# Where the two masked key tiles stand in a flash-attention strip, and how the evacuation of four accumulators is cut in two

## The reference

```
h = layernorm(x)
q, k, v = h @ Wq.T + bq, h @ Wk.T + bk, h @ Wv.T + bv
s = q @ k.T / 32
w = softmax(where(causal, |s|, -inf))          # score * sign(score) = |score|
x = x + layernorm((w @ v) @ Wo.T + bo)
x = x + layernorm(layernorm(x) @ Wfq + fbias + (layernorm(x) @ a) @ b)
```

## The kernel before, in words

| strip | nt | last pieces, by position |
|---|---|---|
| 1 | 4 | 1: lnattn_a(0), lnattn_b(0); 2: outproj(1), lnattn_a(1), ln2t(0), xa(0); 3: ffn(0), lnattn_b(1), lnffn(0) |
| 2 | 6 | 3: outproj(1), lnattn_a(1); 4: ln2t(0), xa(0), ffn(0), lnattn_b(1); 5: lnffn(0) |
| 3 | 8 | 5: ln2t(0), xa(0); 6: ffn(0), lnattn_b(1), lnffn(0) |
| 4 | 10 | 7: xa(0), ffn(0); 8: lnattn_b(1), lnffn(0) |
| 5 | 12 | 9: ffn(0), lnattn_b(1); 10: lnffn(0) |
| 6, 7, 8 | 14, 16, 18 | lnffn(0) at 11, 13, 15 |
| 9 to 15 | 20 to 32 | lnffn(0) at 16, 18, 20, 21, 23, 25, 26 |

## Time and profile before

### The profile page before, as it was taken

One profiled execution on the slowest core, in us unless ns is written; L12 is line 12 of the kernel. 1 busy time (PEld: TensorE's weight loads), 2 busy tenths in 40 slices (PEclk: granted clock), 3 DMA queues, 4 the chain that ended last, 5 costly groups with the idle time before them and its releaser, 6 DMA issues.

```text
span 3685.8 us, 57317 instructions; the slowest of 8 cores (3636.0 to 3685.8 us)
## 1 busy us (share of the span) xinstructions
PE 2705.2 (73%) x17129; PEld 1633.3 (44%) x17129; DVE 1365.5 (37%) x2102; ACT 1406.2 (38%) x3137; POOL 407.2 (11%) x728
## 2 busy tenths in 40 slices
PE   2279888566777778888837988856677777878884
PEld 1234333233445555566513433323344555556661
DVE  3335555344444333333342112034444433333333
ACT  0055453233333344444414545323333344444441
POOL 0000001000111111111100000000011111111110
PEclk9999999778898999999958999967878999999996
DMA  5622222321322323333313222232132232333330
GB/s 148 200 92 92 88 87 84 108 66 58 100 84 89 106 91 111 111 114 109 95 63 126 81 69 69 77 107 66 51 102 83 87 95 95 118 97 122 107 112 18
DMA packets 96560, 348.18 MB, mean 94 GB/s; under 512 B 16245, under 2 KB 16373, under 8 KB 94858
## 3 DMA queue, kind: packets, MB, share of 16 engines
q0 software_dynamic: 64112, 226.54, 20.0%
q1 hardware_dynamic: 32154, 117.97, 9.7%
HBM read 266.85 MB, written 77.59 MB: 93 GB/s over the span
## 4 chain that ended last, share of the span: by engine, by line
PE 50%; DVE 18%; ACT 17%; issue 8%; DMA 4%; ACTq 1%; DVEq 1%; POOLq 0%; SPq 0%; POOL 0%
PE SBp L491 11%; PE OTp L911 8%; PE OTp L532 6%; PE SBp L870 6%; DVE sqb L195 6%; DVE stats L192 5%; PE LBp L751 4%; PE EB L751 4%; PE EB L639 3%; PE LBp L639 2%; DVE t L661 2%; ACT PT L891 2%; ACT Sa L878 2%; ACT stats L203 2%; ACT stats L201 2%
## 5 line engine op out<-in xcount | busy, mean ns | idle before, releaser
L911 PE MATMUL OTp<-PT,V_buf 128*128 128x256 bf16 x4352 | 627.9, 293 | 369.3 <-ACT PT L891 369.0
L870 PE MATMUL SBp<-Qs,Ktr 128*128 128x256 bf16 x4352 | 611.4, 288 | 114.2 <-DVE rl L609 62.9
L911 PEld LDWEIGHTS OTp<-PT,V_buf 128*128 128x128 bf16 x4352 | 439.7, 104 | 485.6 <-issue 411.7
L491 PE MATMUL SBp<-lnT,wsl 128*128 128x512 bf16 x2048 | 485.6, 402 | 76.9 <-ACT Qs L498 44.0
L870 PEld LDWEIGHTS SBp<-Qs,Ktr 128*128 128x128 bf16 x4352 | 410.6, 102 | 235.9 <-issue 159.6
L932 POOL DMA_DIRECT2D Ktr<-k_scr x544 | 299.5, 551 | 1896.8 <-PE SBp L870 1746.2
L208 DVE TENSOR_TENSOR stats<-stats 128x1 f32<-128x1 f32 x256 | 40.8, 159 | 936.5 <-ACT stats L206 928.3
L491 PEld LDWEIGHTS SBp<-lnT,wsl 128*128 128x128 bf16 x2048 | 207.8, 102 | 349.4 <-issue 137.4
L878 ACT ACTIVATE Sa<-SBp 128x256 f32<-128x256 f32 x544 | 209.1, 384 | 295.2 <-PE SBp L870 261.8
L192 DVE TENSOR_REDUCE stats<-t 128x1 f32<-128x1024 f32 x160 | 195.2, 1220 | 260.5 <-ACT t L766 239.4
L891 ACT ACTIVATE PT<-Sa 128x256 bf16<-128x256 f32 x544 | 226.6, 417 | 155.2 <-ACT Sa L878 91.4
(11 more groups left out here) (110 smaller groups left out, 2752.8 us busy)
## 6 DMA issues: line engine op xcount, KB each, us to landing
Ktr<-k_scr POOLq DMA_DIRECT2D x544, 256.0 KB, 3.0
xb<-x SPq DMA_DIRECT2D x128, 512.0 KB, 3.6
y<-xb POOLq DMA_DIRECT2D x64, 512.0 KB, 3.9
q_scr<-Qs POOLq DMA_DIRECT2D x32, 512.0 KB, 4.7
k_scr<-Ktr POOLq DMA_DIRECT2D x64, 256.0 KB, 2.8
Qs<-q_scr SPq DMA_DIRECT2D x32, 512.0 KB, 5.4
xb<-fk SPq DMA_DIRECT2D x8, 512.0 KB, 5.5
xb<-wo SPq DMA_DIRECT2D x8, 512.0 KB, 6.3
```

Source lines behind the costliest of these rows:

```text
L491: E("tensor", lambda e, wreg=wreg, kc=kc, dc=dc, bk_=bk_: e.matmul(out=SBp[:, bk_ * 512:bk_ * 512 + 512], lhsT=wsl[:, wreg * 8192 + dc * 1 ...
L870: E("tensor", lambda e, pos=pos, dc=dc, sp=sp, qof=qof: e.matmul(out=SBp[:, sp * 512:sp * 512 + 256], lhsT=Ktr[:, (pos % 4) * 1024 + dc * ...
L911: lst=(last and vc % 2 == 1): e.matmul(out=OTp[b_][:, col:col + 256], lhsT=V_buf[:, tile * 1024 + vc * 128:tile * 1024 + (vc + 1) * 128], ...
```

## The change

The reordering of tiles is dropped: position j now holds tile j, so the two diagonal tiles stand at the last two positions of the strip instead of the first two. And `pre` is cut: `t_rl` and the evacuations of accumulators 0 and 1 stay at the strip's start, those of accumulators 2 and 3 (`pre2`) are issued behind `emit_S(0)`. The core of the diff; `pos` is renamed `j` throughout.

```
-                for b_ in range(4):
+                for b_ in range(2):
                     pre.append(t_otevac(b_))
+                pre2 = [t_otevac(2), t_otevac(3)]
...
-                    if tile >= 2 * s:
-                        r = E("vector", lambda e, sp=sp, ms=(tile - 2 * s): e.tensor_tensor(
+                    if j >= 2 * s:
+                        r = E("vector", lambda e, sp=sp, ms=(j - 2 * s): e.tensor_tensor(
...
-                order = [2 * s, 2 * s + 1] + list(range(0, 2 * s))
-                for pos in range(nt):
-                    tile = order[pos]
-                    st["ks"][pos] = dma("gpsimd", KS[pos % 4], lambda e, seq=seq, pos=pos, tile=tile: e.dma_start(
-                        out=Ktr[:, (pos % 4) * 1024:(pos % 4 + 1) * 1024], in_=k_scr[seq, tile]),
-                        waits=[(PE, st["pe_slot"][pos % 4])])
-                    emit_S(pos, tile)
-                    if pos > 0:
-                        emit_PV(pos - 1, order[pos - 1])
+                for j in range(nt):
+                    st["ks"][j] = dma("gpsimd", KS[j % 4], lambda e, seq=seq, j=j: e.dma_start(
+                        out=Ktr[:, (j % 4) * 1024:(j % 4 + 1) * 1024], in_=k_scr[seq, j]),
+                        waits=[(PE, st["pe_slot"][j % 4])])
+                    emit_S(j)
+                    if j == 0:
+                        for f in epi_pre2:
+                            f()
+                        epi_pre2 = []
+                    if j > 0:
+                        emit_PV(j - 1)
```

More of the change, by code:

```diff
@@ L831, in make_epilogue @@
                 st["store1_thunk"] = store_stage(1)
-                return pre, main, spill
+                return pre, pre2, main, spill
             epi_pre = []
+            epi_pre2 = []
             pend = []
@@ L875, in emit_S @@
                             waits=w if dc == 0 else (), incs=[(PE, 1)] if dc == 7 else ())
-                    st["pe_slot"][pos % 4] = PE.n
+                    st["pe_slot"][j % 4] = PE.n
                     pe_sT = PE.n
@@ L894, in emit_S, with emit_PV @@
                         waits=wexp, incs=[(AC, 1)])
[L895 to L901, removed]
+                    ac_exp[j] = r[AC]
+                def emit_PV(j):
+                    sp = j % 2
+                    last = (j == nt - 1)
+                    frst = (j == 0)
+                    w = [(AC, ac_exp[j])]
                     first = True
@@ L925, in emit_PV @@
                             waits=wl_, incs=[(PE, 1)] if qc == 1 else ())
-                    pe_pv[pos] = PE.n
+                    pe_pv[j] = PE.n
                     st["pe_pv_slot"][sp] = PE.n
-                order = [2 * s, 2 * s + 1] + list(range(0, 2 * s))
-                for pos in range(nt):
-                    tile = order[pos]
-                    st["ks"][pos] = dma("gpsimd", KS[pos % 4], lambda e, seq=seq, pos=pos, tile=tile: e.dma_start(
-                        out=Ktr[:, (pos % 4) * 1024:(pos % 4 + 1) * 1024], in_=k_scr[seq, tile]),
-                        waits=[(PE, st["pe_slot"][pos % 4])])
-                    emit_S(pos, tile)
-                    if pos > 0:
-                        emit_PV(pos - 1, order[pos - 1])
-                    while popped < n_pend and int(pend[popped][0] * nt) <= pos:
+                for j in range(nt):
[3 more added lines that the diff above has]
+                    emit_S(j)
+                    if j == 0:
+                        for f in epi_pre2:
+                            f()
+                        epi_pre2 = []
+                    if j > 0:
+                        emit_PV(j - 1)
+                    while popped < n_pend and int(pend[popped][0] * nt) <= j:
                         pend[popped][1]()
                         popped += 1
-                emit_PV(nt - 1, order[nt - 1])
+                emit_PV(nt - 1)
                 while popped < n_pend:
```

33 lines of the change are left out of this document (16 added, 17 removed).

## The result

The changed kernel took 3756.39 us (median of 9 runs, lowest 3743.43) against 3691.1 us for the kernel before, run beside it on the same chip: a ratio of **1.0182, 95% interval 1.0160 to 1.0204**, so slower by 1.6 to 2.0%. Some executions of either kernel show a lower granted clock on one half of the chip and take some per cent longer; ratios leave these out, the two medians here do not. The forecast was 3745 us, 1.0173 times its own base of 3681.26. The profiled execution took 3743.43 us, 56.1 more than the 3687.3 of the profile before.

The account below looks back on a forecast made before the run. The path was taken to run through PE, and through ACT and DVE where PE waits. Starts +2.8 and ends +29.2 a sequence, doubled, gave +64 us: 3751 profiled, 3745 predicted as the median; range 3710 to 3780.

Parts of the forecast that it names:

- the order alone: Diagonal tiles last, evacuations uncut: starts win 9 a sequence, ends lose 29.2; 2 x 20.2 = +40 us.
- the cut: Strip starts: evacuations 2 and 3, 1.33 us, now stand between exp and ln2t(1)'s evacuations, which xa(1) waits for.
- Mask adds at the ends: Strip ends: mask adds now delay the last exps, often queued behind layer norms on DVE; +29.2 us a sequence.
- Six strips at 2.73: Ends of strips 3 to 8: add waits behind lnffn(0) up to L786, delaying the value product; 16.4 us a sequence.
- Mask add off the start: Strip starts: exp follows abs by 0.20 instead of 0.87 us; 0.67 won, 0.43 duration, the rest two hand-overs.
- Strip 1: outproj(0) 2.8 us later, 1.0 regained, so start +1.8; end +1.1.
- Rival B: Strips 12 to 15 start at PE's lower clock level after longer idle time; +23 us more, 3768; chance 0.22.
- Rival C: Mask adds find DVE free, so each strip end costs only 0.67 us; +26, 3707 us; chance 0.11.
- rival D: Layer norm before `t_rl` covers strip ends, so only shorter starts count; −20 to −24, 3659 us; chance 0.05.
- the two waits of strip 4: Strip 4's end: one add waits for L786, +2.73; position 8's add holds up lnattn_b(1) until abs, +4.5.

Follow-up runs that it names:

- order_only: Kernel before with the diagonal tiles at the last two positions, evacuations uncut; ratio 1.0057.
- after_nomask: Changed kernel without its 64 mask adds, diagonal tiles unmasked; ratio 1.0030 to the kernel before.
- after_s4: Changed kernel with lnattn_b(1) one position earlier in strip 4 alone, ahead of the mask add; 3737.93 us in one profiled run, no ratio.
- before_nomask: Kernel before without its 64 mask adds, diagonal tiles unmasked; ratio 0.9926.
- split_only: Kernel before with only the evacuations cut in two, diagonal tiles still at positions 0 and 1; ratio 1.0167 (1.0075 to 1.0259).
- split_fill: Kernel before with the evacuations cut in two and zero-tile matmuls in PE's waits; ratio 1.0067.
- mid_7: Kernel before with the diagonal tiles at positions 1 and 2 in strips 7 to 15 only, evacuations uncut; ratio 0.9936.
- mid_all: Kernel before with the diagonal tiles at positions 1 and 2 in strips 1 to 15, evacuations uncut; ratio 0.9961.
- delay1: Kernel before with evacuation 3 done a second time behind each strip's first exp; 3722.87 and 3726.37 us against 3693.3, no ratio.
- fill_zero: Kernel before with zero-tile matmuls added into the accumulators in PE's waits, strips 1 to 8; 3662.25 and 3686.82 us against 3691.1, no ratio.
- mid7_fill: Kernel before with diagonal tiles at positions 1 and 2 from strip 7 on, plus zero-tile matmuls in PE's waits; 3641.65 us, ratio 0.9872.

## Why the prediction was right

- *Sum.* Forecast +64 us; the medians differ by 65.3, the profiled executions by 56.1, and the strips by 58.5 (33.3 and 25.2). The total is better than its parts: by the prediction's terms the order alone was to cost 40 us and the cut 24 on top, and order_only and after put them at 21 and 46 (25 and 34 by the strip sums). Two errors of 10 to 22 us, of opposite sign, nearly cancel, and that is luck.
- *What came as the prediction had it.* L678 starts near the place named, strip 4 takes 8.0 and 6.9 us more, exp's wait for the mask add goes from 48.5 to 88.0 us, xa(1) comes 0.7 later in strips 2 to 6. *What did not:* strips 10 to 15 were each to change by under 1 us; strip 11 of the first sequence took 2.8 more, and strip 14 took 3.5 less, for the reason given under the table.
- *Mask adds at the ends, +58.* Right in kind, and right or somewhat too large (45 by the strip sums, 56 by the ratios of after and after_nomask): strip 4's timeline shows both waits where they were put, +7.13 against 7.2, and after_s4 takes the second alone away.
- *Six strips at 2.73.* The wait is there in all six: over the last two value products it grows by 2.4 to 3.2 us in strips 5 to 8 of the first sequence and by 2.2 to 3.2 in the second, in strips 6 to 8 ahead of the last but one. But it is not always in the strip's time. End of strip 3, core 1, first the kernel before, then after:

```profile
855.45 0.42 ACT L891 ACTIVATE PT<-Sa 128x256 bf16<-128x256 f32 x1 [0.20 <-ACT Sa L878]
856.01 1.23 PE L911 MATMUL OTp<-PT,V_buf 128*128 128x256 bf16 x5 [7.15 <-ACT PT L891]
```

```profile
848.25 0.42 ACT L893 ACTIVATE PT<-Sa 128x256 bf16<-128x256 f32 x1 [2.91 <-DVE Sa L887]
848.82 1.01 PE L913 MATMUL OTp<-PT,V_buf 128*128 128x256 bf16 x4 [9.86 <-ACT PT L893]
```

  The wait is 2.71 us longer, as forecast. Yet strip 3 took only 1.5 us more, since its score product behind ffn(1)'s first half ran in 1.05 us instead of 1.89, the value product in 1.04 instead of 1.92 and the second half in 1.89 instead of 2.55. These three products were 2.4 us shorter behind an xa(1) that waited 2.66 us instead of 2.35.
- *Mask add off the start.* 0.67 us each is right in the rows of strips 2 to 6 (0.20 against 0.87 behind abs). It is 0.43 of the add's own time and one hand-over of some 0.24 us more than before, not two. Whether the term's sum was too small is not settled (27 us by before_nomask, with 20 inside its interval).
- *The cut.* This term was too small: 24 to 30 us counted for the cut by itself, 34, 42 and 47.5 by the strip sums of three pairs of kernels. The delay of xa(1) is exact (0.67 in strip 5 of after with the mask add gone, 1.34 in split_only with it in place). What I left out is what PE's level does behind it. In strip 5 of after, core 1, xa(1) waits 2.66 us instead of 1.99, and the end of ffn's first half comes 12.43 us behind the reciprocal instead of 10.11: 2.3 us later, where the walk has 0.67. And from strip 12 on, abs of position 1 stands behind the moved evacuations, as split_only shows in strip 13.
- *Strip 1.* Its 2.9 came out (+3.0 and +2.7), but by luck. outproj(0) was to start 2.8 us later, because I took abs at 669.14, its time behind four evacuations. With two in front abs starts sooner, and outproj(0) is only 1.45 us later on core 1 (4.12 us behind the reciprocal against 2.67), 1.8 as the median over the cores. What makes up the rest of the strip's 3 us was not traced.
- *Rival B* (strips 12 to 15 at the lower level, +23) did not come: the clock of strips 10 to 15 is 0.96, and the first score product of strips 12 to 15 takes 1.03 us as before in six of the eight (1.34 and 1.47 in the other two, as medians over the cores); these strips change by −4.1 and +1.9. The Trainium skill (TensorE: Matmul & The Clock Gate, "HAM oscillation — how this bites in real kernels") holds that each long idle gap makes the next burst begin throttled. This case's rows agree in kind in strip 5 (1.89 and 1.92 us behind the 4.17 us gap, 1.05 and 1.04 behind 1.95); but in strip 8 of split_fill the level fell behind a gap of 1.29 us. And they put it into the short strips, where it took time in some and gave it back in others. *Rival C* (0.67 at each end) is refuted by waits of 2.91 us, *rival D* by strips that are longer from one reciprocal to the next, 1 to 11 all of them in the first sequence.

## What to carry to other kernels

When an operation moves in an in-order list, ask who stands ahead of it on its own engine at the new place, and whom it now holds up while it waits; the two waits of strip 4 came from that alone and were the best-sized part of this forecast. A strip's end, where the last exp feeds the last product and the product feeds the next strip, is a poor place for one more hop between engines; place 1 or 2 was better in strips 7 to 15 (mid_7), while in strips 1 to 6 it won nothing (mid_all). And where PE runs in bursts between waits, a shift of half a microsecond on another engine may cost or give 2 to 4 us at PE: read the durations of the first products behind each wait, not the idle time alone.

## What the runs showed of the hardware that was not expected

- A delay of 0.67 us a strip on ACT (delay1) took 36 us over 30 strips in its profiled execution, 1.2 each, spread as jumps of 3 to 5 us in some strips and nothing in others.
- Two kernels with the same lists up to strip 6 (fill_zero and mid7_fill) differ by 4.7 us in one of these strips. And taking work away made a strip 4.2 us longer (strip 6 of before_nomask).
- One program showed both outcomes on different cores at once: strip 4 of after_nomask took 67.4 or 71.2 us in the first sequence, and nothing between.
- Matmuls of zeros, 88.1 us in all, made the kernel some 0.6% faster (0.9936 to 0.9872) with the granted clock at 1.00 over the waits that they fill, where it was read (strip 5 of fill_zero); the core's mean clock went from 0.884 to 0.891 (mid_7) to 0.899 to 0.906 (mid7_fill).
- Left open: whether a fill ahead of xa(1) takes back what the cut costs. It was not run.
